# New order tables for all five engines of a gated attention and expert kernel

## The reference

```python
def reference(x, ctx, g_xattn, g_ffn, Wq, bq, Wk, bk, Wv, bv, Wo, bo, router_w, router_b, expert_w, expert_b):
    x = x + tanh(g_xattn[0]) * cross_attention(layernorm(x), ctx)   # 16 heads of 32
    x = x + tanh(g_ffn[0]) * experts(layernorm(x))
    return x

# cross_attention
scores = einsum('bhqd,bhkd->bhqk', Q, K) / sqrt(32)
attn = softmax(scores, axis=-1)
ctx = einsum('bhqk,bhkd->bhqd', attn, V)
return ctx @ Wo.T + bo

# experts: the one with the largest router probability, of 8
probs = softmax(xt @ router_w + router_b, axis=-1)
gate = max(probs); idx = argmax(probs)
y = gate[:, None] * (xt @ expert_w[idx] + expert_b[idx])
```

## Time and profile before

| | |
|---|---|
| runs before | 1144.06, 1184.27, 1148.18; median 1148.18 |
| the profiled execution | span 1149.5, mean granted clock 0.966 |
| PE busy | 1021.9 (89% of the span) |
| DVE, ACT, POOL busy | 804.2 (70%), 513.6 (45%), 671.0 (58%) |
| first Q matmul of batches 0 to 7 | 30.2, 130.6, 241.4, 353.3, 465.6, 577.1, 688.8, 801.5 |
| first and last expert matmul | 988.82 and 1136.7 |

### The profile page before, as it was taken

One profiled execution on the slowest core, in us unless ns is written; L12 is line 12 of the kernel. 1 busy time (PEld: TensorE's weight loads), 2 busy tenths in 40 slices (PEclk: granted clock), 3 DMA queues, 4 the chain that ended last, 5 costly groups with the idle time before them and its releaser, 6 DMA issues. The chain is left out here.

```text
span 1149.5 us, 19046 instructions
## 1 busy us (share of the span) xinstructions
PE 1021.9 (89%) x5464; PEld 650.7 (57%) x5464; DVE 804.2 (70%) x1748; ACT 513.6 (45%) x920; POOL 671.0 (58%) x446
## 2 busy tenths in 40 slices
...
GB/s 233 76 75 119 69 80 70 141 77 98 66 140 78 89 84 129 75 84 85 138 66 84 108 124 79 72 119 102 77 64 88 234 102 83 156 130 147 137 123 54
DMA packets 70884, 119.39 MB, mean 104 GB/s; under 512 B 17854, under 2 KB 18878, under 8 KB 70656
## 3 DMA queue, kind: packets, MB, share of 16 engines
...
q10 hardware_dynamic: 2048, 0.53, 0.2%
...
## 5 line engine op out<-in xcount | busy, mean ns | idle before, releaser
L691 ACT ACTIVATE probs<-sc 128x512 f32<-128x512 f32 x512 | 279.3, 598 | 205.2 <-PE sc L499 163.1
L1101 POOL TENSOR_TENSOR psum_keys<-psum_keys,probs 128x1024 f32<-128x1024 f32 x128 | 303.8, 2387 | 109.8 <-ACT probs L691 109.6
L826 DVE TENSOR_REDUCE maxima<-jb 128x1 f32<-128x512 f32 x512 | 322.5, 680 | 61.2 <-PE jb L519 60.4
L1101 POOL TENSOR_TENSOR psum_keys<-probs 128x1024 f32<-128x1024 f32 x64 | 153.5, 2413 | 231.2 <-ACT probs L691 231.2
L519 PE MATMUL jb<-k_stack,q_stack 96*128 96x512 f32 x512 | 192.9, 430 | 25.1 <-issue 9.1
L499 PE MATMUL sc<-q_stack,k_stack 98*128 98x512 f32 x512 | 193.1, 427 | 10.1 <-DMA q_stack<-max_rows 8.3
L509 PE MATMUL hb<-probs,values 128*32 128x512 f32 x1024 | 140.4, 626 | 16.4 <-DVE heads_raw L845 7.9
L519 PEld LDWEIGHTS jb<-k_stack,q_stack 96*128 96x128 f32 x512 | 95.5, 193 | 101.2 <-issue 40.3
L499 PEld LDWEIGHTS sc<-q_stack,k_stack 98*128 98x128 f32 x512 | 95.1, 193 | 83.5 <-ACT probs L691 29.9
L861 DVE SCALAR_TENSOR_TENSOR k_lo<-jb,bias,k_hi 128x512 fp32r<-128x512 f32 x32 | 23.9, 747 | 64.0 <-ACT k_hi L710 64.0
L667 PE MATMUL sc<-e_hi,heads_hi 128*128 x156 | 67.4, 432 | 1.0 <-issue 0.5
...
## 6 DMA issues: line engine op xcount, KB each, us to landing
...
k_stack<-k_lo SPq DMA_DIRECT2D x128, 64.0 KB, 2.0
q_stack<-q_lo SPq DMA_DIRECT2D x128, 64.0 KB, 2.0
...
```

Of the source, the lines that this page charges most:

```text
L691: nc.scalar.activation(probs[:, kt % 2, h, :], scs[(16 * g + n) % NSC][:], ACT.Exp, scale=SCALE)\
L826: nc.vector.tensor_reduce(maxima[g % 2][:, n:n + 1], jbs[j][:], AX.X, ALU.max).then_inc(s["mx_done"], 1)
L1101: nc.gpsimd.tensor_tensor(psum_keys[:, two, :], in0, probs[:, kt % 2, two, :], ALU.add)\
```

## The change

Only the four tables change. The instructions, buffers and semaphores of every step are the same; line numbers fall by 3, because the tables are shorter (line 848 of before is line 845 of the changed kernel). The first lines of the difference, cut to one pair for two of the tables:

```diff
 ORDER = {
     "SP": [
-        "~~RW2 ~~RW3 1SQ ^DC0 1SK 2SQ 2SK ^DC1 ~RW0 ^DC2 ^DC3 ~RW1 ~DR2 ~DR3 3SQ ^DX0 ^DX1 ^DX2 3SK ^DX3 DR0 DR1 ^0SQ",
-        "^0SK",
+        "^DC0 1SQ ~~RW3 1SK ~~RW2 2SQ 2SK ^DC1 ~DR2 ~RW1 ~RW0 ^DC2 ~DR3 3SQ ^DC3 ^DX0 ^DX1 3SK ^DX2 ^DX3 ^0SQ ^0SK DR0 DR1",
...
 OPENING = {
     "SP": [
-        "~RW2 ^DC0 ^DC1 LW1 ^DC2 ~RW3 LC ^DC3 ^DX0 LW0 ^DX1 ^DX2 ^DX3 LW2 LW3 ^0SK ^0SQ",
+        "^DC0 ^DC1 ^DC2 LW1 ^DC3 ^DX0 ^DX1 LW0 LC ^DX2 ^DX3 LW3 LW2 ^0SK ~RW2 ~RW3 ^0SQ",
```

More of the change, by code:

```diff
@@ L34 @@
     "SP": [
-        "~~RW2 ~~RW3 1SQ ^DC0 1SK 2SQ 2SK ^DC1 ~RW0 ^DC2 ^DC3 ~RW1 ~DR2 ~DR3 3SQ ^DX0 ^DX1 ^DX2 3SK ^DX3 DR0 DR1 ^0SQ",
-        "^0SK",
+        "^DC0 1SQ ~~RW3 1SK ~~RW2 2SQ 2SK ^DC1 ~DR2 ~RW1 ~RW0 ^DC2 ~DR3 3SQ ^DC3 ^DX0 ^DX1 3SK ^DX2 ^DX3 ^0SQ ^0SK DR0 DR1",
     ],
     "PE": [
[10 rows of a table removed]
[10 rows of a table added]
     ],
     "ACT": [
[5 rows of a table removed]
[5 rows of a table added]
     ],
     "DVE": [
[5 rows of a table removed]
[5 rows of a table added]
     ],
     "POOL": [
-        "C3 ~1A3 ~~OP2 ~~OP3 ~1A4 ~1A5 LX0 ~2A0 LX1 ~2A1 LX2 LX3 ~2A2 ~OP0 ~2A3 ~2A4 ~2A5 ~~LR1 ~3A0 ~3A1 ~3A2 ~3A3 ~3A4",
-        "~3A5 ~OP1 0A0 0A1 0A2 0A3 0A4 0A5 ~LR0 1A0 1A1 ^C0 ^C1 ^C2 1A2",
+        "~~OP2 ~~OP3 ~1A3 ~1A4 ~1A5 C3 LX0 LX1 ~2A0 ~2A1 LX2 LX3 ~2A2 ~2A3 ~2A4 ~2A5 ~~LR1 ~3A0 ~3A1 ~3A2 ~3A3 ~3A4 ~3A5 0A0",
+        "0A1 0A2 0A3 ~OP0 ~OP1 0A4 0A5 ~LR0 1A0 1A1 ^C0 ^C1 1A2 ^C2",
     ],
@@ L71 @@
     "SP": [
-        "~RW2 ^DC0 ^DC1 LW1 ^DC2 ~RW3 LC ^DC3 ^DX0 LW0 ^DX1 ^DX2 ^DX3 LW2 LW3 ^0SK ^0SQ",
+        "^DC0 ^DC1 ^DC2 LW1 ^DC3 ^DX0 ^DX1 LW0 LC ^DX2 ^DX3 LW3 LW2 ^0SK ~RW2 ~RW3 ^0SQ",
     ],
     "PE": [
[4 rows of a table removed]
[4 rows of a table added]
     ],
     "ACT": [
-        "^C0 ^C1 WT0 TH ^C2 ^C3 WT1 WT2 WT3 ^NX0 WT4 ^0K WT5 WT6 ^NX1 ^T4 ^NX2 ^T5 WT7 ^NX3 ^T6 ^T7 WT8 WT9 WT10 ^0Q WT11",
-        "WT12 WT13 WT14 WT15 ^1Q ^V0 ^0MT ^0MD ^1K ^0E0 ^0E1 ^0E2 ^0E3 ^V1 ^0E4 ^0E5 ^0E6 ^2Q ^0E7 ^V2 ^0E8 ^0E9 ^0E10",
-        "^0E11 ^2K ^0E12 ^0E13 ^0E14",
+        "^C0 ^C1 ^C2 WT0 WT1 WT2 WT3 ^C3 ^NX0 ^NX1 WT4 WT5 ^T4 TH ^T5 ^0K WT6 ^NX2 ^NX3 ^T6 ^T7 WT7 WT8 WT9 ^0Q WT10 WT11",
+        "WT12 WT13 WT14 WT15 ^1Q ^V0 ^1K ^0MT ^0MD ^0E0 ^0E1 ^0E2 ^0E3 ^V1 ^0E4 ^0E5 ^2Q ^0E6 ^V2 ^0E7 ^0E8 ^0E9 ^0E10 ^0E11",
+        "^0E12 ^0E13 ^2K ^0E14",
     ],
     "DVE": [
[3 rows of a table removed]
[3 rows of a table added]
     ],
@@ L96 @@
     "SP": [
-        "~~RW2 ~~RW3 1SQ 1SK ^DC0 ^DC1 2SQ ^DC2 ^DC3 ~DR2 2SK ~RW0 ~DR3 ^DX0 ^DX1 ~RW1 ^DX2 3SQ 3SK ^0SQ ^DX3 ^0SK DR0",
+        "1SQ 1SK ^DX1 ^DC2 ~~RW2 ~~RW3 ^DX3 ~DR2 ^DC0 ^0SK ^DC1 2SQ 2SK ~DR3 ~RW0 ~RW1 DR0 ^0SQ 3SQ 3SK ^DX2 ^DC3 ^DX0",
     ],
     "PE": [
[10 rows of a table removed]
[10 rows of a table added]
     ],
     "ACT": [
[6 rows of a table removed]
[5 rows of a table added]
     ],
     "DVE": [
[5 rows of a table removed]
[5 rows of a table added]
     ],
     "POOL": [
-        "~1A3 C3 ~~OP2 ~~OP3 ~1A4 ~1A5 LX0 ~2A0 LX1 ~2A1 LX2 LX3 ~2A2 ~2A3 ~~LR1 ~OP0 ~2A4 ^LX0 ~2A5 ^C0 ~3A0 ~3A1 ~3A2",
-        "~3A3 ~3A4 ~3A5 0A0 0A1 ~OP1 0A2 0A3 ~LR0 0A4 0A5 ^LX1 1A0 ^C1 ^C2 ~OP2 1A1 1A2 ^C3 ~OP3 1A3 1A4 1A5 2A0 ^LX2 2A1",
-        "^LX3 2A2 2A3",
+        "~1A3 ~~OP2 ~~OP3 ~1A4 ~1A5 LX0 LX1 ^LX2 C3 ~2A0 ~2A1 ^C0 LX2 LX3 ^C3 ~2A2 ~2A3 ~2A4 ~2A5 ^LX3 ~~LR1 ~3A0 ~3A1 ~3A2",
+        "~3A3 ~3A4 ~OP0 ~3A5 0A0 0A1 0A2 ~OP1 0A3 ^LX1 ^C1 0A4 0A5 ~LR0 ^C2 ~OP2 ~OP3 ^LX0 1A0 1A1 1A2 1A3 1A4 1A5 2A0 2A1",
+        "2A2 2A3",
     ],
@@ L134 @@
     "SP": [
-        "W0 ~DR1 ~DR2 W1 W6 W2 W3 W4 W5 ~~RW2 ~DR3 ~~RW3 W7 EB ~RW0 ~RW1 ~RW2 ~RW3",
+        "W0 ~DR2 ~DR1 W1 W2 W6 W5 W7 W4 W3 ~DR3 ~~RW3 ~~RW2 EB ~RW0 ~RW1 ~RW2 ~RW3",
     ],
     "PE": [
[5 rows of a table removed]
[5 rows of a table added]
     ],
     "ACT": [
[4 rows of a table removed]
[4 rows of a table added]
     ],
     "DVE": [
[4 rows of a table removed]
[4 rows of a table added]
     ],
     "POOL": [
[5 rows of a table removed]
[4 rows of a table added]
     ],
```

## The result

The changed kernel took 1137.17 us in the median of 8 runs (1123.39 to 1138.49), the kernel before 1150.18 us (8 runs). The ratio is 0.9874, 95% interval 0.9831 to 0.9917: some 13 us faster, which is within 2% and clear of zero. Later both ran again, the changed kernel at 1151.44 and before at 1157.39, ratio 0.9937 (0.9912 to 0.9962). The forecast of 1122 had the sign and about twice the size. The range 1106 to 1150 held the time, but partly because misses cancelled. In the traces the opening gave 5.2 us instead of 6.5, the steady batches lost 13.0 instead of gaining 9, and the last batch with the expert part gave 21.1 instead of 11.5.

The account below looks back on a forecast made before the run. PE was taken as the bound in steady batches, its work fixed, so the change is worth the PE waits that vanish: 1149.5 - 6.5 - 9 - 11.5 = 1122.5, forecast 1122, range 1106 to 1150.

Parts of the forecast that it names:

- Term 1: Opening: third context tile split ahead of wk brings x loads, Q and first M earlier; 6.5 us saved, bounds 3 to 9.
- The chain I named: Opening: third context split at about 6, next x load at about 8.2, 4.9 us earlier, reaching PE's Q and first M.
- Term 2: Seven steady batches: PE's waits for SUM1, SUM2 and maxima shrink; 1.3 us saved per batch, 9 us in seven.
- The gains I counted: Per steady batch: 0.56 us for SUM2, 0.4 for maxima, 0.3 small waits, 0.3 SUM1, less 0.3 for later layer norm.
- The slower rival: Steady batches: 0NL, now ahead of LX0, meets POOL's sums and PE loses 5.85 us each; 1172, middle 1160; chance 0.12.
- Term 3: End of last batch: long waits behind 1NL and W0 go, 3NM comes 13 us earlier, less 1.7 us; -11.5 us.
- the terms -13 and +1.7: End of last batch: 3NM 13 us earlier, against PE waiting about 1.7 us for the second split of TO14 and TO15.

## Why the prediction was right in sign and twice too large

**Term 1, the opening: right in mechanism, somewhat large.** -4.0 us at the first M and -5.2 at batch 1, for -6.5. The chain I named moved: the split, the x load, Q and the first M all came earlier. The third context tile was split 1.4 us later than I took, and the x tile behind it went out 1.2 us later. But the first M comes at 37.3 to 40.1 us in four traces of the old opening and at 34.1 to 37.5 in ten of the new, so 3 to 4 us is what the traces bear, and by itself this table is worth nothing that the times show.

**Term 2, the steady batches: wrong, by 22 us.** The gains I counted came: no wait of SUM1 or SUM2 in batches 2 to 5 of the changed kernel (before 0.65 and 0.57 us per batch), half of the one for the maxima of group 3 (0.89 to 0.41). The step that failed is the cost of nothing for what lies between MT and the first score. I costed MT's new neighbours on PE only, and left out the queues that it passes: RT1 on ACT in front of 1MT (1.24 us instead of 0.3) and SP's loads, now issued in the transfer's microsecond. That 1MT goes ahead of RT1 again takes the whole wait of group 1 away. For group 2 I had LR2 on DVE in front of 2MT in mind; putting that back left the wait as it was, so its cause stays open. The prediction's text names the wait for the maxima that travel by DMA, and lets it shrink by 0.4 us; it shrank by 0.5 at group 3 and grew from nothing to 2.2 us at group 1 and 1.2 at group 2. And such waits cost more than themselves: of the 13.0 us only 4.2 are idle time. The prediction took PE's busy time as fixed; in all it nearly was (1021.9 and 1019.9), but mostly because 8.8 us more in the steady batches met 8.6 less in the last one. In batch 2 PE waited 2.85 us at 309.8, and the next steps started 0.43 us apart instead of 0.23, the lower clock level.

The slower rival (0NL meets POOL's run) is what happened on DVE: 2.65 to 4.07 us in batches 1 to 6 where it gave 2 to 7. Its price for PE was too high, for the split lost one sum, or a sum and a context split, and not three: putting it back was worth 10.5 us of the steady stretch in one trace, not 41. The chance of 0.12 that I gave it was for its full price; as a partial loss it was likely, since the rows showed POOL busy until 449.04 and the split starting at about 447.

**Term 3, the last batch: right up to 3NM, but by two misses that cancelled.** From 1M12 to the first expert matmul the traces have -15.2 us, from the first Q of batch 7 -17.9; by the times, the two tables alone are worth 10 us, for -11.5 (the terms -13 and +1.7 make -11.3). 3NM came 13.9 us earlier, counted from 1M12; I had 13. That is luck: MT came 12.8 us earlier where I had 5.85, 2NM 15.4 where I had 10, and the start of PA 22.0; then PA, which I had left at its old length, paid 8.2 us to POOL's work and gave the excess back. 2NL met POOL and paid for one sum (2.21 us), as taken. TO15 waited 3.7 us, against 1.7 taken. But "1NL is behind all sixteen maxima, so PE does not wait for it; only MT does" failed in its second half: MT is on PE's path, by the transfer to the first score. The wait of 8.84 holds 3 to 4 us of 1NL (with 1NL elsewhere it was 5.1 to 5.7) and some 3 us of a transfer that is slow beside the expert weights, a price that I put at nothing. What made the stretch shorter is what followed: W0 and W1 filled DVE's idle time before 2SC, 3P0 no longer waited 5.4 us, and of the 14.2 us 8.6 are less busy time, in part by the clock.

**The page's rule.** The Trainium skill, "SBUF — State Buffer", section "SBUF: two separate sides", lets the one that starts first keep the shared ports for its whole instruction; so a meeting should cost at most the rest of one sum. In this case the splits at 933.57 (2.21 us) and 677.10 (2.65 us) agree. Those at 912.25, 913.76 and 896.20 (7.25, 5.14 and 3.37 us) do not: each ended only behind the last of a row of sums, and so behind one or two more sums than the one it met. Why a waiting DVE instruction gets its turn after one sum in some places and not in others stays open.
